# Six GpSimd drains among 74 gathers, in place of twenty memsets: a recommendation model's forward pass

## The reference

```
wide = dense @ Wd_wide
for si, wi in zip(S, w):
    wide = wide + wi[si]
wide = wide + wc0[S[3] * VOCABS[4] + S[4]]
wide = wide + wc1[S[5] * VOCABS[6] + S[6]]
deep_in = concatenate([dense @ Wd_deep] + [Ei[si] ...], axis=1)   # 2048 x 576
h = relu(deep_in @ W1)      # 576 -> 512
h = relu(h @ W2)            # 512 -> 256
return bias + h @ W3 + wide # 2048 x 1
```

## Time and profile before

| | |
|---|---|
| executions | 128.6, 130.53, 131.19 us; median 130.53 |
| profiled execution | 129.13 us, of which 127.3 us span from first to last instruction |
| TensorE (PE) busy | 117.8 us, 92% |
| GpSimd (POOL) busy | 104.8 us, 82% |
| VectorE (DVE) busy | 80.7 us, 63% |
| ScalarE (ACT) busy | 57.1 us, 45% |
| mean granted TensorE clock | 0.979 |

### The profile page before, as it was taken

The page is one execution under the profiler, slowest core; times in us unless marked ns, Lnnn a source line. Parts: engine busy times, 40 slices in busy tenths (PEclk is TensorE's granted clock), DMA queues, the critical chain, the costliest instruction groups (busy, mean ns, idle before and its releaser), DMA issues.

```text
span 127.3 us, 1843 instructions
## 1 busy us (share of the span) xinstructions
PE 117.8 (92%) x630; PEld 89.2 (70%) x630; DVE 80.7 (63%) x188; ACT 57.1 (45%) x100; POOL 104.8 (82%) x146
## 2 busy tenths in 40 slices
PE   6979999988999999999999999999999999999710
PEld 2443886646688885788788885787888867888710
DVE  2695996998999604975999025695995040257510
ACT  3599777456946052345462151509170432063200
POOL 6488888888899889888898888898898888888800
PEclk9999999999999999999999999999999999999965
DMA  3957766668922322223233322200000000000000
GB/s 118 344 60 248 147 178 74 133 89 323 290 21 24 26 21 21 21 19 23 21 26 20 21 20 22 21 0 0 6 0 0 0 3 0 6 0 0 0 3 0
DMA packets 6049, 7.48 MB, mean 59 GB/s; under 512 B 2755, under 2 KB 3939, under 8 KB 6040
## 3 DMA queue, kind: packets, MB, share of 16 engines
q0 software_dynamic: 2368, 1.62, 17.6%
q1 hardware_dynamic: 3240, 5.03, 12.1%
q10 hardware_dynamic: 432, 0.72, 1.6%
HBM read 7.17 MB, written 0.19 MB: 58 GB/s over the span
## 4 chain that ended last, share of the span: by engine, by line
POOL 79%; issue 11%; DMA 4%; POOLq 1%; DVE 1%; DVEq 0%
POOL x_pair L333 26%; POOL pause_sb L326 21%; POOL cross L351 18%; POOL x_two L341 14%; DMA idx_raw<-in_index_dram 2%; DMA cross<-in_wc_dram,idx_cross 2%; POOLq L100 1%; DVE idx_wrap L497 0%; DVE idx_sum L499 0%; DVE idx_look L502 0%; DVE result L702 0%; DVE idx_gather L502 0%; DVEq L701 0%
## 5 line engine op out<-in xcount | busy, mean ns | idle before, releaser
L517 DVE TENSOR_SCALAR onehot<-idx_bc,row_id 128x512 fp32r<-128x512 f16 x76 | 39.4, 583 | 3.7 <-PE io_ps L742 2.6
L333 POOL DMA_INDIRECT x_pair<-in_rows_dram,idx_gather x32 | 33.2, 1038 | 8.0 <-issue 6.2
L351 POOL DMA_INDIRECT cross<-in_wc_dram,idx_cross x26 | 25.4, 978 | 4.3 <-issue 4.3
L326 POOL MEMSET pause_sb<- 128x320 f32 x61 | 26.6, 437 | 0.0
L786 PE MATMUL l_ps<-xt_hi,w_hi 128*128 128x512 f32 x64 | 25.8, 404 | 0.2 <-DVE xt_lo L537 0.2
L788 PE MATMUL l_ps<-xt_hi,w_lo 128*128 128x512 f32 x64 | 25.1, 392 | 0.0
L787 PE MATMUL l_ps<-xt_lo,w_hi 128*128 128x512 f32 x64 | 25.0, 390 | 0.0
L730 PE MATMUL io_ps<-onehot,table_hl 128*128 128x512 f32 x76 | 21.0, 406 | 0.1
L375 ACT CAST xt_hi<-io_ps 64x512 fp32r<-64x512 f32 x20 | 11.6, 580 | 19.8 <-PE io_ps L730 19.6
L537 DVE TENSOR_TENSOR xt_lo<-io_ps,xt_hi 128x512 fp32r<-128x512 f32 (+1 forms) x8 | 5.5, 688 | 23.6 <-ACT xt_hi L388 23.6
L341 POOL DMA_INDIRECT x_two<-in_rows_dram,idx_gather x16 | 17.7, 1104 | 3.2 <-issue 3.2
(11 more groups left out here) (89 smaller groups left out, 132.4 us busy)
## 6 DMA issues: line engine op xcount, KB each, us to landing
idx_bc<-idx_dram SPq DMA_DIRECT2D x3, 640.0 KB, 6.2
table<-in_wc_rows_dram SPq DMA_DIRECT2D x1, 564.0 KB, 4.1
w_sb<-in_w_dram ACTq DMA_DIRECT2D x2, 256.0 KB, 4.6
x_pair<-in_rows_dram,idx_gather POOLq DMA_INDIRECT x32, 3.6
w_sb<-in_w_dram SPq DMA_DIRECT2D x2, 256.0 KB, 3.5
w_sb<-in_w_dram SPq DMA_DIRECT2D x1, 512.0 KB, 4.1
dense_stack<-dense_dram SPq DMA_DIRECT2D x3, 156.0 KB
table<-in_small_dram SPq DMA_DIRECT2D x1, 416.0 KB, 3.8
```

The lines of the kernel that those rows point to most:

```text
L326: nc.gpsimd.memset(pause_sb[:], 0.0).then_inc(paused, 1)
L333: nc.gpsimd.indirect_dma_start(out=x_pair[:, t, g * ROW:(g + 1) * ROW], out_offset=None, in_=big[g], in_offset=bass.IndirectOffsetOnAxis(a ...
L351: nc.gpsimd.indirect_dma_start(out=cross[:, c, t:t + 1], out_offset=None, in_=wc[c], in_offset=bass.IndirectOffsetOnAxis(ap=idx_cross[:, c ...
L517: nc.vector.tensor_scalar(onehot[:, CHUNK0[i] + c, :], idx_bc[:, b % (BLOCKS - 1), i, :], row_id[:, c:c + 1], None, ALU.is_equal).then_inc ...
```

## The change

`pause` gives way to `rest(n)`, called behind every one of the 74 gathers with the running count n. Behind gathers 12, 24, 36, 48, 60 and 72 GpSimd runs a `drain` instruction. Behind the first eight of each twelve from gather 13 on it runs the memset of before, with the same wait; behind the ninth, tenth and eleventh of each twelve it runs nothing. The first eleven gathers keep nothing behind them. So 42 memsets stay (40 in five full twelves, and behind gathers 73 and 74), 15 are dropped, 5 are replaced by a drain, the drain behind gather 12 stands where nothing stood, and the memset behind gather 74 is new.

```diff
-            def pause(n):
-
-                if n:
-                    pool.wait_ge(paused, n)
-                nc.gpsimd.memset(pause_sb[:], 0.0).then_inc(paused, 1)
+            pauses = [0]
+
+            def rest(n):
+
+
+                if n % (NG * BT) == 0:
+                    nc.gpsimd.drain()
+                elif n > NG * BT and n % (NG * BT) <= NG * BT - 4:
+                    if pauses[0]:
+                        pool.wait_ge(paused, pauses[0])
+                    nc.gpsimd.memset(pause_sb[:], 0.0).then_inc(paused, 1)
+                    pauses[0] += 1
 
             pool.wait_ge(gather_index_ready, 1)
-            pauses = 0
+            gathers = 0
...
-                        if b > 0:
-                            pause(pauses)
-                            pauses += 1
+                        gathers += 1
+                        rest(gathers)
...
-                    if (c, t) != (NX - 1, TILES - 1):
-                        pause(pauses)
-                        pauses += 1
+                    gathers += 1
+                    rest(gathers)
```

## The result

The changed kernel takes 144.16 us in the median of four executions (142.79 to 145.66), the kernel before 130.51 us. The ratio is 1.106, with a 95% interval of 1.092 to 1.121. (Ratios here are formed over executions that lie within 1.5% of the fastest; medians are over all.) The forecast was 127.0 us, with a range of 125.3 to 137.0: wrong in sign and outside the range. The profiled execution took 145.66 us, with a span of 143.9.

A forecast was written before the change was run, and what follows sets the result against it. GpSimd's closing drain was taken to set the end, 2.8 us after SP. With the last gather at 6 x 1.16 - 7.8 = -0.84 us and SP's store ending the span, 130.53 - 3.5 = 127.0 us; range 125.3 to 137.

The forecast's parts named there:

- What bounds the kernel: At the end of the span: GpSimd's closing drain sets the end, 2.8 us after SP.
- The formula 6D - 7.8: Shift of the last gather in us: six gaps D with drains, less dropped and replaced memsets; forecast -0.84 us.
- What is D: Time from a gather's end to the next gather's start with a drain between them; taken as 1.16 us.
- leftovers by count: At each drain: it clears 0.083 us per gather since the last drain, 1.0 us behind twelve; the reading taken.
- a fixed price: At each drain: any drain behind a gather costs 6.12 us; last gather +28.9 us, 159.4 us in all; chance 0.17.
- the wait for landing: At each drain: it waits for gathered data to land, 2.65 us behind gathers 12 to 48, 1.35 behind 60 and 72.
- The memsets' terms: In GpSimd's gather stream: 15 memsets dropped save 4.5 us, 5 replaced by drains give 5D - 3.0.
- Cover of the later gathers: Blocks 1 and 3: last pair gathers have 8.6 and 24 us to spare, so delays of 5.8 and 15.1 us fit.
- The landing rival: Inner drains wait for data to land: last gather +5.5 us, end +2.7, 133.2 us; chance 0.14.
- The queue at a fixed pace: Gather leftovers are served at 1.657 us each, drains move the waiting into the stream: 133.1 to 140.6 us; chance 0.16.
- The leftover stays with the last gather: Inner drains cost about 1.2 us or less, the closing one still 6.12 us; typically 128.7 us; chance 0.13.
- the queue's worst: In the gather stream: the fixed-pace server also idles one 1.25 us step after each drain, +10 us, 140.6 us.

The follow-up runs named there:

- Experiment 5: The changed kernel with each of its six drains replaced by a GpSimd wait for the landing of all gathers so far: 140.6 us.
- 4: The kernel before with one drain, behind gather 36, in place of its memset: 132.9 us, ratio 1.013.
- 9: The kernel before with one drain, behind gather 12, all memsets kept: 136.6 us, ratio 1.056.
- 10: The kernel before with one drain, behind gather 60, in place of its memset: 134.2 us.
- experiment 3: The kernel before with no memset and no drain behind any gather: 192.1 us.
- 6: The kernel before with memsets of 4 columns in place of 320, each still waiting for the one before it, no drains: 190.0 us.
- 7: The kernel before with memsets of 4 columns, each to its own columns and with no wait between them, no drains: 184.6 us.
- experiment 8: The kernel before without memsets or drains; from gather 13 on GpSimd waits for VectorE's one-hot builds instead: 150.4 us.
- 2: The changed kernel's memset pattern with the drains left out: 133.7 us.
- 11: The kernel before with memsets 256 columns wide in place of 320, no drain: 130.1 us.
- 12: The kernel before with memsets 192 columns wide in place of 320, no drain: 133.1 us.

## Why the prediction was wrong

**What bounds the kernel: right.** The end hung on GpSimd's closing drain, 2.8 us behind SP. It fell away in the changed kernel, and SP ends the span. The close itself had been put at 0.17 us past the last gather; it ended 1.45 past it, 0.98 up to the last packet and 0.47 more, by the same mistake as the inner drains.

**The formula 6D - 7.8 for the last gather: right in form.** With the measured gaps it gives 13.6 of 19.5 us. The missing 5.9 are, on balance, GpSimd instructions that got longer, three of them by 7.2 us together; the prediction had no term for this.

**What is D: this step failed.** The prediction set three readings side by side (leftovers by count, a fixed price, the wait for landing) and took one. Behind twelve gathers two of them hold at once and add up, and a third piece, the restart of the gathers, was mis-sized. Over the six drains of the changed kernel: from the gather's end to the last packet 3.0, 2.3, 2.1, 2.3, 1.1, 1.1, together 11.9 us; from there to the drain's end 0.8 to 1.0 each, 5.1 together; from there to the next gather's start, the restart, 0.73 each, 4.4 together, where the gap of 0.17 behind a memset had been put. The leftover by count was the reading taken, and its size was about right: 1.0 forecast for twelve gathers, 0.8 to 1.0 measured past the last packet. What was missing was the landing, put at nothing: 11.9 of the 21.4 us. It was set aside because the closing drain's 6.12 us didn't fit a wait for data. But that drain had 74 gathers to clear, and its 6.12 us stayed the same wherever the last packet stood, so it could say nothing about a drain with twelve, where the landing is the larger piece. Experiment 5 shows the landing by itself, 4, 9 and 10 show the count.

**The memsets' terms: wrong in what they leave out.** Twenty fewer memsets were booked as -7.5 us (-4.5 and -3.0) at no cost, as nobody reads what they write. On GpSimd that holds. But experiments 3, 6, 7 and 8 show that the other engines run late when gathers step by 1.42 us or less on average, or in long bursts (experiment 8: 1.60 on average, 1.25 within a burst), with waits put down to "remote" of up to 42.8, 39.4, 29.7 and 10.8 us; at 1.52 to 1.57 (experiments 2, 11 and 12) the profiled executions do so by 4 to 8 us. In the changed kernel this cost hardly shows: the drains slow the gathers anyhow, to 1.84 us a step. TensorE's path is 1.7 us longer than before (last matmul at 122.62), and 1.6 of them arise by 12.1 us, ahead of the first drain (the matmul that starts at 12.09 started at 10.48 before); VectorE then waits 18 us for the last gather anyway.

**Cover of the later gathers: right.** Block 1 and block 3 were not held up; TensorE's path ended by 123.2, though block 3's last pair gather started 15.6 us later than before (89.00 against 73.41).

**The rivals.** The landing rival came closest in mechanism, with +2.7 us against the measured +13.6. Adding to its +5.5 the count (5.1) and the restart (6 x 0.73) gives +15.0 for the last gather, where the formula with the measured gaps gives +13.6 and the trace +19.5. That the medians differ by the same 13.6 as the formula gives is chance. The fixed price is refuted by the close, 0.47 us past the last packet with two gathers. The queue at a fixed pace is refuted by the same row, and by experiment 3, where the close ends at 110.0 instead of 127. Its suspicion that the pace matters was sound, though for the other engines, not for the drain. "The leftover stays with the last gather" is refuted too.

**The chances.** Slower by over 2% had 0.39 and faster 0.34. The range reached to 137.0 and left out the full-price case and the queue's worst; nearly every case was a single cause, and none added the landing to the count.

**What stays open.** What a drain does in the 0.05 to 0.08 us a gather is not in the records; no row of GpSimd or of its queue stands in that time. In these runs only drains reset the count: after 74 gathers with memsets or waits between them the close took 4.9 us or more past the last packet, behind a drain two gathers earlier 0.45 and 0.47. The exact form in which count and landing combine is open too, as the drain after 36 gathers shows. The count can't be told apart from the number of rows either, as every gather here has 128. Why the other engines start late where gathers step fast is open as well: the records of experiment 3 show the lookup's end at 60.7 and the semaphore's event at 111.76, just before ScalarE's late start, not what lies between. Some records of semaphores are missing in those traces, so a wait put down to "remote" may not name its cause. A drain whose leftover is spread over stretches where GpSimd has nothing to do could not be tried: this kernel's gathers fill GpSimd's time from 4.5 us to the end.

## What to carry to other kernels

A drain of GpSimd in this stream of gathers was a full stop: price one like it as the last gather's landing (1.1 to 3.0 us to the last packet in the changed kernel), plus the leftover of all gathers since the last drain (0.8 to 1.0 us for twelve, 3.9 for 60), plus the restart (0.73 us), and not by the 0.19 us of the opening drain. A cause that can't be seen in one wait may still be the larger part of another that is shorter (here the landing, 11.9 of 21.4 us), so price the sum of the causes before dropping any. A filler instruction that nobody reads may be pacing its engine for the sake of the others (here 131.0 us with the memsets and 192.1 without); take it away in an experiment, with the other engines' last instructions in view, before booking its time as a gain.

## What the runs showed of the hardware

- A drain of GpSimd ended 0.5 us past the last packet with 2 gathers since the last drain, 0.8 to 0.9 with 12 (0.97 to 1.20 behind the first twelve), 0.95 with 14, 1.8 with 36, 2.1 with 38, 3.9 with 60, 4.2 with 62, 4.9 to 5.2 with 74 with memsets, waits for VectorE or nothing between the gathers (5.4 with landing waits, 6.0 in one kernel with short memsets). After 74 it ended 6.12 us past the last gather's end in six kernels, wherever the last packet stood. The next gather started 0.72 to 0.73 us after it in every one of 15 cases.
- In kernels whose 128-row gathers stepped by 1.30 or 1.42 us on average, single waits of ScalarE and VectorE lasted up to 43 us, and the executions 181 to 209 us in place of 130. At 1.52 to 1.57 us TensorE's path was 4 to 8 us longer in the profiled executions; at the 1.59 us of the kernel before, ScalarE's longest wait was 4.5 us, and for TensorE.
- Eight one-hot builds on VectorE took 4.18 us with gathers and memsets of GpSimd running between them, and 3.24 us beside one gather that took 4.63 us in place of 0.95 (4.46 to 6.59 us in four other profiles).
